# Graph attention kernel: the matrix that carries sums between node spans, made by ScalarE as an eighth one-hot

## What is computed

```python
e = (left + right + em_e) / 3.0
e = jnp.where(e > 0, e, NEG_SLOPE * e)
e_max = jax.ops.segment_max(e, dst, num_segments=N)
e_exp = jnp.exp(e - e_max[dst])
e_sum = jax.ops.segment_sum(e_exp, dst, num_segments=N)
a = e_exp / e_sum[dst]
msg = feat_src[src] * a[:, :, None]
rst = jax.ops.segment_sum(msg, dst, num_segments=N)
```

## Time and profile before

| | us |
| --- | --- |
| median of 3 runs | 2975.55 (2974.45 to 2976.66) |
| the profiled execution, its own time | 2972.55 |
| its span | 2970.7 |
| busy in the span: PE | 2640.5 (89%) |
| DVE | 2221.8 (75%) |
| ACT | 1676.1 (56%) |
| POOL | 1985.5 (67%) |

### The profile page before, as it was taken

The page is one execution under the profiler, slowest core; times in us unless marked ns, Lnnn a source line. Parts: engine busy times, 40 slices in busy tenths (PEclk is TensorE's granted clock), DMA queues, the critical chain, the costliest instruction groups (busy, mean ns, idle before and its releaser), DMA issues.

```text
span 2970.7 us, 49107 instructions
## 1 busy us (share of the span) xinstructions
PE 2640.5 (89%) x13426; PEld 1859.5 (63%) x13426; DVE 2221.8 (75%) x7629; ACT 1676.1 (56%) x3730; POOL 1985.5 (67%) x2041
## 2 busy tenths in 40 slices
PE   7699999999999899789999998899999988888884
PEld 5477777777677677466666665566666556655552
DVE  6369999999999999556666666566666647877885
ACT  5357777778777787355554553455555434434430
POOL 3576777767667776177776665777766657777772
PEclk9699999999999999799999999999999999999995
DMA  8767787777777777377776655777666567777762
GB/s 231 216 197 211 225 237 229 230 230 229 228 225 222 229 231 231 119 232 228 224 220 198 209 172 170 227 219 230 214 204 197 151 202 229 247 245 239 234 211 67
DMA packets 455093, 630.37 MB, mean 212 GB/s; under 512 B 94496, under 2 KB 373088, under 8 KB 454816
## 3 DMA queue, kind: packets, MB, share of 16 engines
q0 software_dynamic: 97184, 280.55, 33.4%
q1 hardware_dynamic: 325568, 301.63, 32.7%
q10 hardware_dynamic: 32064, 44.98, 4.2%
HBM read 551.28 MB, written 75.63 MB: 211 GB/s over the span
## 4 chain that ended last, share of the span: by engine, by line
PE 43%; DVE 36%; issue 7%; POOL 6%; ACT 3%; DMA 2%; DVEq 0%; SPq 0%; POOLq 0%; ACTq 0%
PE ps L1303 21%; DVE cell_marks L2090 6%; DVE ring L2019 6%; PE ps L1355 5%; PE ps L1377 4%; DVE lane_marks L2091 4%; POOL ring L1248 4%; PE ps L1341 4%; PE ps L1315 3%; DVE block_cube L804 2%; POOL ring L621 2%; PE ps L1881 2%; DVE block_ey L1993 2%; DVE block_inv_norm L806 2%; DVE attention_work L1996 2%
## 5 line engine op out<-in xcount | busy, mean ns | idle before, releaser
L1248 POOL DMA_INDIRECT ring<-message_table,src_index x1209 | 1181.6, 977 | 556.3 <-issue 379.7
L621 POOL DMA_INDIRECT ring<-attention_table,src_index x784 | 777.7, 992 | 308.0 <-issue 225.0
L1303 PE MATMUL ps<-count_rows,high_rows 128*128 128x512 f32 x1764 | 756.5, 429 | 99.7 <-ACT attention_work L1635 71.4
L1303 PE MATMUL ps<-count_rows,low_rows 128*128 128x512 f32 x1764 | 717.4, 407 | 0.0
L1645 ACT ACTIVATE count_rows<-one_hot 128x512 fp32r<-128x512 uint8 x882 | 524.6, 624 | 182.7 <-PE ps L1303 171.4
L1303 PEld LDWEIGHTS ps<-count_rows,high_rows 128*128 128x128 f32 x1764 | 345.2, 196 | 213.5 <-issue 92.8
L1881 PE MATMUL ps<-ring,one_hot 128*128 128x265 f32 x1568 | 438.6, 404 | 2.2 <-issue 2.1
L1524 DVE CAST high_rows<-attention_work 128x512 fp32r<-128x512 f32 x441 | 194.4, 441 | 287.1 <-PE ps L1303 267.8
L1303 PEld LDWEIGHTS ps<-count_rows,low_rows 128*128 128x128 f32 x1764 | 345.8, 196 | 74.5
L1881 PEld LDWEIGHTS ps<-ring,one_hot 128*128 128x128 f32 x1568 | 304.7, 201 | 63.5 <-issue 8.2
L1526 DVE TENSOR_TENSOR low_rows<-attention_work,high_rows 128x512 fp32r<-128x512 f32 x441 | 309.9, 703 | 15.2
(11 more groups left out here) (199 smaller groups left out, 3624.1 us busy)
## 6 DMA issues: line engine op xcount, KB each, us to landing
attention_work<-message_table SPq DMA_DIRECT2D x432, 256.0 KB
one_hot<-dense_adjacency SPq DMA_DIRECT2D x126, 448.0 KB, 4.2
attention_work<-in_dst_edges SPq DMA_DIRECT2D x112, 448.0 KB
ring<-message_table,src_index POOLq DMA_INDIRECT x1209
dense_adjacency<-root ACTq DMA_DIRECT2D x24, 784.0 KB, 6.1
attention_sums<-sums_out SPq DMA_DIRECT2D x112, 132.5 KB
ring<-attention_table,src_index POOLq DMA_INDIRECT x784
message_table<-attention_work ACTq DMA_DIRECT2D x98, 128.0 KB, 2.9
```

Of the source, the lines that this page charges most:

```text
L621: pool.indirect_dma_start(m.ring[:, k, t, 0:cols], None, table, bass.IndirectOffsetOnAxis(ap=m.src[:, at:at + 1], axis=0)).then_inc(s[f"ro ...
L1248: pool.indirect_dma_start(m.quad_ring[:, k, j, :], None, m.tables[w.l], bass.IndirectOffsetOnAxis(ap=m.src[:, t:t + 1], axis=0)).then_inc( ...
L1303: last = nc.tensor.matmul(m.ps[:, 2 + half, 0:cols], rows[:, v % SPLITS, half * P:(half + 1) * P], m.a_rows[:, k, 0:cols], start=(j == 0 a ...
```

## The change

The eighth matrix of a chunk, the one with `shift_by`, is made by ACT in `own_side(c)` behind the seven `Abs`, by the same two operations: `Abs` of `shift_by[c]` less `step`, and then `Relu` of 1 less that. It goes into an eighth place of `one_hot`; the one `Relu` for the chunk runs over 1024 columns, not 896, except for chunk 0. `shifting`, its 111 instructions L2011, its semaphore and `shift_mat` are gone, and PE's product waits only for `kept`, since the wait for `onehot` stands ahead of the chunk's first product. `one_hot` is 1024 bytes larger a partition, and the 1024 bytes of `shift_mat` are free.

```diff
@@ sum_tiles (PE)
                 pe.wait_ge(s["kept"].sem, s["kept"].done(c - 1))
-                pe.wait_ge(s["shifted"].sem, s["shifted"].done(c - 1))
-                last = nc.tensor.matmul(sums, m.shift_mat[:, parity, :], m.sums_out[:, 1 - parity, :],
+                last = nc.tensor.matmul(sums, m.one_hot[:, parity, TILES, :], m.sums_out[:, 1 - parity, :],
                                         start=False, stop=True)
@@ DVE
-        def shifting(c):
-
-            if c >= 2:
-                dve.wait_ge(s["summed"].sem, s["summed"].done(c - 2))
-            nc.vector.tensor_scalar(m.shift_mat[:, c % 2, :], m.step[:], m.shift_by[:, c:c + 1], None,
-                                    ALU.is_equal).then_inc(s["shifted"].sem, 1)
@@ the steps of DVE
             for n in at_step(c, 0):
                 node(n)
-            if 0 < c < CHUNKS:
-                shifting(c)
@@ own_side (ACT)
+            made = TILES
+            if c:
+                last = nc.scalar.activation(m.one_hot[:, c % 2, TILES, :], m.step[:], ACT.Abs,
+                                            bias=m.shift_by[:, c:c + 1], scale=-1.0)
+                made = TILES + 1
             last.then_inc(s["apart"].sem, 1)
             act.wait_ge(s["apart"].sem, s["apart"].done(c))
-            nc.scalar.activation(m.one_hot[:, c % 2], m.one_hot[:, c % 2], ACT.Relu, bias=1.0, scale=-1.0).then_inc(s["onehot"].sem, 1)
+            nc.scalar.activation(m.one_hot[:, c % 2, 0:made], m.one_hot[:, c % 2, 0:made], ACT.Relu, bias=1.0, scale=-1.0).then_inc(s["onehot"].sem, 1)
@@ build
-        m.one_hot = sb("one_hot", [P, 2, TILES, P])
-        m.shift_mat = sb("shift_mat", [P, 2, P])
+        m.one_hot = sb("one_hot", [P, 2, TILES + 1, P])
```

More of the change, by code:

```diff
@@ L1684 @@
     edges1=None, edges2=None, edges3=None, edges4=None, edges5=None, distance=0, oht=0, right=1, kinds=1, masked=0,
-    scored=0, leaky=0, xt=1, bwd=0, mt=1, diff=1, expd=2, denoms=0, weighed=0, apart=0, onehot=0, shifted=0, summed=2, kept=1,
+    scored=0, leaky=0, xt=1, bwd=0, mt=1, diff=1, expd=2, denoms=0, weighed=0, apart=0, onehot=0, summed=2, kept=1,
     store0=None, store1=None, sums=None, recips=0, norm=0, x1=0, stats=0, mv=0, newton=0, inv_norm=0, shift=0,
@@ L2473, in build @@
         m.root = sb("root", [P, BLOCKS, D])
-        m.one_hot = sb("one_hot", [P, 2, TILES, P])
-        m.a_small = m.one_hot[:].rearrange("p k t e -> p (k t e)").bitcast(uint8).rearrange("p (g k n) -> p g k n", g=BUNCHES, k=HALF // STRIPE)
-        m.shift_mat = sb("shift_mat", [P, 2, P])
+        m.one_hot = sb("one_hot", [P, 2, TILES + 1, P])
+        m.a_small = m.one_hot[:].rearrange("p k t e -> p (k t e)").bitcast(uint8)[:, 0:BUNCHES * HALF // STRIPE * BUNCH * STRIPE] \
+            .rearrange("p (g k n) -> p g k n", g=BUNCHES, k=HALF // STRIPE)
         m.sums_out_t = sb("sums_out", [P, 2, SUMC])
```

## The result

The changed kernel took 2948.75 us in the median of 6 runs (2946.24 to 2957.72); the kernel before, beside it on the same chip, 2976.11 (2971.43 to 2979.49, 6 runs). The medians differ by 27.4 us, where 18.5 were forecast. The ratio on record is 0.9915, 95% interval 0.9898 to 0.9931; it isn't the quotient of the two medians (0.9908) and stands for 25 us.

A forecast was written before the change was run, and what follows sets the result against it. DVE was taken to bound the attention loop: 2972.55 - 19.2 (removal) + 0.5 (stores) + 0.2 (loop's end) = 2954.1 us. The saving of 18.5 off the median 2975.55 gave 2957 us, range 2951 to 2968.

The forecast's parts named there:

- The bound: Attention loop, 226 to 1157 us: DVE, busy 96%, sets the pace of the 96 steps; PE is busy 93%.
- (a): PE takes over in part of the attention loop's steps; 7 us of the gain lost, 2964 us; chance 0.12.
- (c): PE or POOL holds the pace throughout the attention loop; no change, 2974 to 2977 us; chance 0.09.
- The removal: On DVE in the attention loop, dropping L2011 saves 0.20 us a step, 19.2 us in 96 steps.
- (e): L2011's whole duration, 0.28 us a step, goes on DVE; 2949 us; chance 0.03.
- (b): L2011's place on DVE is not taken at once, saving 0.08 us a step; 2969 us; chance 0.07.
- The addition: On ACT in own_side, eighth Abs and wider Relu add 0.40 us a step, 38 us in 96 steps, covered.
- (d): ACT becomes the pace setter, DVE's L2019 waiting for its exponentials; slower, 2985 us; chance 0.03.
- The cover: ACT's waits and the exponentials' 1.33 us lead over DVE's product hide ACT's extra work; 0.73 us stays.
- The stores: Behind ACT's waits for stores into dense_adjacency, DVE's saving returns as its own wait; 0.5 us of gain lost.
- The loop's end: Past 1157 us, ACT's 0.40 us counts once, less 0.20 of DVE: +0.2 us.
- five terms: Bound, removal on DVE, addition on ACT, stores and loop's end; the sum was 2972.55 - 19.2 + 0.5 + 0.2 us.

The follow-up runs named there:

- lag pair: One-column memset on POOL ahead of each chunk's gathers, added to the kernel before and to the changed kernel: 2972.51 and 2953.87 us.
- doubled: Kernel before with a second instruction equal to L2011 ahead of it in each step, into a spare array: 2986.09 us, ratio 1.0047.
- lanes_on_act: Changed kernel with two of a step's eight lane marks made by ACT, one Relu for both: 2934.68 us.
- act_only: Kernel before with ACT's eighth Abs and wide Relu added, their result unread: 2975.50 us, median of nine runs, ratio 1.0006.
- shift_early: Kernel before with L2011 moved on DVE from the step's end to between the product and the marks: 2969.46 us, ratio 0.9997.
- after_again: The changed kernel run once more, unchanged: 2955.3 us, median of 4 runs.
- dve_only: Changed kernel without ACT's eighth matrix; PE's product takes the identity, so carried sums land at wrong rows: 2950.32 us.
- lag_after: Changed kernel with a one-column memset on POOL ahead of each chunk's gathers: 2953.87 us.
- lane_on_act: Changed kernel with one of a step's eight lane marks made by ACT: 2935.25 us.

## Why the prediction was right or wrong

**The bound: right.** DVE kept its 96% and the front of each step began without a pause behind it; PE's rise to 95% cost no wait of DVE. Rivals (a) and (c) ask for waits of DVE for L1868 or L1847, and DVE stood idle for 0.7 us in all. By the first half of the rule of the Trainium skill ("Perfetto Trace Analysis", Identifying the Most-Contended Engine), with PE as the engine to work on, nothing was to be gained; the trace decides for its second half. The waits of PE that the profile put down to `one_hot` have no line at all in after, though the `Relu` now ends later. That fits what the prediction read in the code, that L1928 doesn't wait for it.

**The removal: right in its size.** 18.9 us in 95 steps against 19.2 in 96. What comes back elsewhere was put at nothing; with the marks equal the lag pair nets 17.1. The doubled kernel gives 0.197 us apiece, which rules out (e), and the distances 0.35 and 0.07 rule out (b).

**The addition: right.** The `Abs` was put at 0.29 to 0.31; it starts 2.04 us behind the first of seven, which is 0.29 between starts. The `Relu` rose from 0.95 to 1.06, in the middle of 0.09 to 0.14. ACT's waits shrank and DVE's did not grow; the kernels with one half of the change each say the same from both sides, and lanes_on_act shows where (d) begins. The cover is thinner than forecast: where no wait for a store stands ahead, 0.73 us were to stay between the end of the exponentials (L2161 after) and the product's start, and the tightest such step of after, at 876.0 us, has 0.46.

**The stores: a wrong sign.** A loss of 0.5 us was set against the gain. ACT waited 7.8 us for them and not 13.2, and the product's 1.04 us of waits in the stretch went. The error is 1.5 us, and act_only, shift_early and doubled, with 0.89, 0.41 and 0, show that it varies.

**The loop's end: small as said.** From step 103 to step 111 it took 54.29 us before and 53.69 after, against +0.2 forecast. What lies behind step 111 is the same code and took 1757.5 to 1766.1 us over fourteen profiles, which by itself is as wide as the error of the forecast. The granted clock there was 0.937 in the longest and 0.941 in the shortest, but the order isn't strict.

**The step that failed** is none of the five terms but the form of the sum: 2972.55 less the terms takes every other instruction of DVE at what one profiled execution shows, and the range counted only the bounds of the terms. The cell marks weren't looked at, as their code is unchanged. They carry 9 to 19 us of meetings with the gathers (67 to 152 marks of 0.12 us), and their number changes between kernels, and between two executions of after from 84 to 129. In the profiled pair that is 8.0 us, partly taken back by 2.3 of other lengthening; with L2011's 18.9 these give the 24.6. Eight us more below would have put the range's low end at 2943, and 2948.75 inside.

So the size of the miss is in part luck: the same two kernels differed by 18.3 us in the repeat.

**What stays open.** What sets the number of long marks isn't settled. All six profiles with a shorter step that gather on POOL have 67 to 129 (after, after_again, dve_only, lag_after, lane_on_act, lanes_on_act), the five with the old one 136 to 152. So a part of the extra may well belong to the change, through the step's length. The doubled kernel, with a longer step and 76, shows that it isn't a matter of shorter alone. How many marks fall 0.5 to 0.7 us behind a gather's start decides most of it (in these twelve profiles 1295 of the 1567 such marks are long, and only 148 of all others), but why so many fall there in one kernel and so few in another was not traced. The repeat puts the change at 18.3 us and the first set at 27.4; all that is shown is that in the profiled pair the part above 19 us comes from the marks, and that it isn't steady. The 3.4 us between the first set's 27.4 and its profiled pair's 24.0 have no trace: before's profiled run lay 3.6 below the median beside it, and no slower run was profiled.

## What to carry to other kernels

Price a small instruction by the distance from its start to the next start, not by its duration, and look for the engine that sets the pace stage by stage. Before giving a range, list the instructions whose code is unchanged but whose durations have two values in the trace, and ask what they meet: where the number of meetings can vary, it belongs into the range. When work is handed to an engine with time to spare, go on until waits for it come back: here it held for one more piece and ended with the second.

## What was not expected of the hardware

- An f16 `tensor_scalar` of 392 columns on DVE takes 0.12 us more when it starts 0.4 to 0.8 us behind the start of an indirect DMA of 0.95 us on POOL, while one of 128 columns keeps its distance to the next start. With as many rows loaded by plain DMAs from SP it never does (0 of 760 twice).
- A second identical `tensor_scalar` of 128x128 f32 adds 0.197 us a step, though each lasts about 0.3: neighbours on DVE overlap by a third of their time.
- The same program differs by 12 us between executions (2946.24 to 2958.36), and its two profiled ones by 4.2 us in the 95 steps and by 5.7 behind them. In the 95 steps the cell marks grew by 5.4 us and other lines gave 1.2 back; the 5.7 has no explanation here.
